# Channel-norm variance in four column groups of 32, root and reciprocal over 128 partitions

## What is computed

```
x1 = depthwise_conv3x3(x) + dw_b                   # NHWC: 128 channels last
mu = x1.mean(-1, keepdims=True)
var = ((x1 - mu) ** 2).mean(-1, keepdims=True)     # one value per pixel, over 128 channels
x1 = (x1 - mu) / jnp.sqrt(var + LN_EPS) * ln_g + ln_b
x1 = jax.nn.gelu(x1, approximate=False)
offset = x1 @ off_w + off_b                        # and a softmax mask, also from x1
```

## Time and profile before

| | |
|---|---|
| median of 3 runs | 10189.35 us (10180.25 to 10204.99) |
| the profiled execution | 10212.5 us |
| its span, first to last instruction | 10210.4 us |
| mean granted clock of TensorE, 1 is full speed | 0.891 |
| period of a sample in the loop | about 590 to 604 us |

### The profile page before, as it was taken

One profiled execution on the slowest core, in us unless ns is written; L12 is line 12 of the kernel. 1 busy time (PEld: TensorE's weight loads), 2 busy tenths in 40 slices (PEclk: granted clock), 3 DMA queues, 4 the chain that ended last, 5 costly groups with the idle time before them and its releaser, 6 DMA issues.

```text
span 10210.4 us, 287594 instructions
## 1 busy us (share of the span) xinstructions
PE 8259.8 (81%) x123582; PEld 4592.7 (45%) x123582; DVE 7412.6 (73%) x8864; ACT 3945.7 (39%) x6092; POOL 211.1 (2%) x253
## 2 busy tenths in 40 slices
PE   6468888887888888788888878888887888888796
PEld 5324435353444535344343535434353443535354
DVE  2487777778777776877777687777768777786863
ACT  0034434253443425344342534435253443435332
POOL 0000000000000000000000000000000000000000
PEclk7579898998989899899989989899998989899898
DMA  4001101111110111111011111101111110111101
GB/s 111 6 13 35 47 20 45 37 37 39 41 47 20 45 37 37 39 41 47 20 45 37 37 39 41 47 20 45 37 37 39 41 46 20 45 32 43 41 24 52
DMA packets 230313, 391.71 MB, mean 38 GB/s; under 512 B 25200, under 2 KB 166480, under 8 KB 221776
## 3 DMA queue, kind: packets, MB, share of 16 engines
q1 hardware_dynamic: 229008, 372.66, 13.1%
HBM read 192.47 MB, written 130.55 MB: 32 GB/s over the span
## 4 chain that ended last, share of the span: by engine, by line
PE 58%; DVE 22%; issue 11%; ACT 7%; DMA 1%; DVEq 0%; POOL 0%; SPq 0%; ACTq 0%; POOLq 0%
PE ps L881 10%; PE ps L686 7%; PE ps L750 7%; DVE arena L1703 4%; PE ps L783 4%; PE ps L981 4%; PE ps L758 3%; PE ps L799 3%; PE ps L971 3%; DVE arena L1758 3%; PE ps L707 3%; PE ps L772 2%; DVE arena L1680 2%; DVE arena L1686 1%; DVE arena L1798 1%
## 5 line engine op out<-in xcount | busy, mean ns | idle before, releaser
L881 PE MATMUL ps<-arena,ident 64*64 64x512 f32 x5600 | 1761.5, 679 | 743.5 <-DVE arena L1703 740.4
L883 PE MATMUL ps<-arena,ident 48*64 48x512 f32 x5600 | 1765.5, 679 | 0.0
L1703 DVE TENSOR_TENSOR arena<-arena 112x2560 f32<-112x2560 f32 x560 | 1578.4, 2820 | 99.5 <-PE ps L883 93.1
L881 PEld LDWEIGHTS ps<-arena,ident 64*64 64x64 f32 x5600 | 493.2, 148 | 1785.1 <-issue 1774.4
L750 PE MATMUL ps<-arena,wqk 128*128 128x400 f32 x2048 | 926.9, 572 | 170.8 <-DVE arena L1807 108.5
L686 PE MATMUL ps<-vp,convw 128*128 128x448 f32 x2016 | 819.5, 549 | 23.6 <-ACT vp L1300 23.6
L1792 DVE COPY arena<-ps 128x400 f32<-128x400 f32 x512 | 293.3, 573 | 728.3 <-PE ps L750 728.1
L1686 DVE TENSOR_TENSOR arena<-arena 112x576 f32<-112x576 f32 x1008 | 764.1, 758 | 34.9
L799 PE MATMUL ps<-arena 64*64 64x33 f32 x32768 | 652.6, 230 | 116.4 <-issue 58.8
L783 PE MATMUL ps<-ident,arena 128*128 128x128 f32 x4096 | 594.9, 292 | 150.9 <-ACT arena L1097 43.7
L1798 DVE TENSOR_REDUCE arena<-ps 128x16 f32<-128x800 f32 x512 | 505.2, 987 | 282.2 <-PE ps L772 278.0
(11 more groups left out here) (294 smaller groups left out, 12637.3 us busy)
## 6 DMA issues: line engine op xcount, KB each, us to landing
windows_out<-arena SPq DMA_DIRECT2D x1024, 100.0 KB
arena<-windows_out SPq DMA_DIRECT2D x224, 256.0 KB, 4.1
arena<-windows_out SPq DMA_DIRECT2D x224, 192.0 KB, 3.4
arena<-in_wqk SPq DMA_DIRECT2D x16, 2048.0 KB, 8.5
arena<-in_x_t SPq DMA_DIRECT2D x16, 1568.0 KB, 10.1
arena<-in_x SPq DMA_DIRECT2D x16, 1568.0 KB, 7.7
arena<-arena SPq DMA_DIRECT2D x32, 784.0 KB
out_x<-xb SPq DMA_DIRECT2D x112, 224.0 KB, 2.0
```

Source lines behind the costliest of these rows:

```text
L881: nc.tensor.matmul(ps[half, 3, :], ident[0:SLOT, 0:SLOT], prod[0:SLOT, ring(c, dy), dx, :], start=(s < 2), stop=(s >= TAPS - 2), skip_grou ...
L883: mm = nc.tensor.matmul(ps[half, 4, :], ident[SLOT:PT, SLOT:], prod[SLOT:PT, ring(c, dy), dx, :], start=(s < 2), stop=(s >= TAPS - 2), ski ...
L1703: V.tensor_tensor(prod[0:PT, ring(c, dy), :, :].rearrange("p k (n e) -> p k n e", e=CG), taps.to_broadcast([PT, SHIFTS, N64, CG]), for_tap ...
```

## The change

The seven variance matmuls no longer write seven partitions of one tile. Chunk k writes to the 32 partitions from 32 (k % 4), the column group k % 4. The weight is one of two 128x32 matrices: for chunks 0 to 3 the columns 0 to 15 hold 1/128 and the rest zero, for chunks 4 to 6 the columns 16 to 31. So each variance row exists 16 times, and chunk k's is at partition 32 (k % 4) + 16 (k // 4). Chunks 0 to 3 start the accumulation in their column group, chunks 4 to 6 add to it; group 3 has chunk 3 alone, and its other 16 partitions hold zero.

The square root and the reciprocal go over all 128 partitions. The spread matmul of chunk k contracts over the 32 partitions of its quarter, with the one-hot column of `ident` that picks the row. Order, semaphores, banks, and the number of matmuls stay.

```diff
-        varsel = sb("varsel", [C, CHUNKS, CHUNKS])
+        varsel = sb("varsel", [C, 2, 32])
...
             def spread_rows(n, k, bank):
                 pe.wait_ge(ln_r.sem, ln_r.at(n))
-                nc.tensor.matmul(ps[:, bank, 0:CH], ident[0:CHUNKS, k:k + 1].to_broadcast([CHUNKS, C]),
-                                 var_rows[0:CHUNKS, :], start=True, stop=True).then_inc(bc_p.sem, 1)
+                quarter, at = slice(32 * (k % 4), 32 * (k % 4) + 32), 32 * (k % 4) + 16 * (k // 4)
+                nc.tensor.matmul(ps[:, bank, 0:CH], ident[quarter, at:at + 1].to_broadcast([32, C]),
+                                 var_rows[quarter, :], start=True, stop=True).then_inc(bc_p.sem, 1)
...
                     for k in range(CHUNKS):
-                        mm = nc.tensor.matmul(ps[0:CHUNKS, 5, 0:CH], varsel[:, k, :], y1[:, k * CH:(k + 1) * CH],
-                                              start=(k == 0), stop=(k == CHUNKS - 1))
+                        quarter = slice(32 * (k % 4), 32 * (k % 4) + 32)
+                        mm = nc.tensor.matmul(ps[quarter, 5, 0:CH], varsel[:, k // 4, :], y1[:, k * CH:(k + 1) * CH],
+                                              start=(k < 4), stop=(k >= 3), skip_group_check=True)
                     mm.then_inc(ln_v.sem, 1)
...
                     act.wait_ge(ln_v.sem, ln_v.at(n))
-                    nc.scalar.activation(sd_rows[0:CHUNKS, :], ps[0:CHUNKS, 5, 0:CH], ACT.Sqrt, bias=eps_col[0:CHUNKS, :]
-                                         ).then_inc(ln_d.sem, 1)
+                    nc.scalar.activation(sd_rows, ps[:, 5, 0:CH], ACT.Sqrt, bias=eps_col[:, :]).then_inc(ln_d.sem, 1)
...
-            V.memset(varsel[:, :, :].rearrange("p a b -> p (a b)")[:, 0:CHUNKS * CHUNKS:CHUNKS + 1], 1.0 / C)
+            for hv in range(2):
+                V.memset(varsel[:, hv, 16 * hv:16 * hv + 16], 1.0 / C)
...
                     dve.wait_ge(ln_d.sem, ln_d.at(n))
-                    V.reciprocal(var_rows[0:CHUNKS, :], sd_rows[0:CHUNKS, :]).then_inc(ln_r.sem, 1)
+                    V.reciprocal(var_rows, sd_rows).then_inc(ln_r.sem, 1)
```

## The result

| | before | after |
|---|---|---|
| median of the runs | 10190.6 us (4 runs, 10180 to 10205) | 10057.0 us (4 runs, 10053 to 10121) |
| ratio of after to before, 95% interval | | 0.9883 (0.9841 to 0.9924) |
| profiled execution: span, mean granted clock | 10210.4 us, 0.891 | 10051.0 us, 0.903 |

134 us less, 1.3%.

A forecast was written before the change was run, and what follows sets the result against it. TensorE was taken to lead (81% busy), alone in the variance step. Direct gain 15 x 3.7 + 4.0 + 2.2 = 61.7 us plus 87 us of clock falls, off the median 10189.35, gave 10041 us; range 9995 to 10145.

The forecast's parts named there:

- Variance step: Fourteen variance matmul passes, four column groups at once: 5.43 to 1.67 us, counted as 3.7 us less per sample.
- The table load: Before the square root: its 1.28 us load delays the root, so the matmul waiting on it starts at most 0.3 us later.
- The estimate from the Trainium skill's figure for three groups: Variance step: 2.38 times faster, 5.36 to 2.3 us, 3.1 us less per sample, 46 us over 15 samples.
- Root and reciprocal over 128 partitions: Square root and reciprocal after the variance step: 128 instead of 7 partitions cost between 0 and 0.05 us.
- Sample 0: First sample, at low clock: variance step 4.0 us less, three spread pairs 2.2 us less.
- The falls behind spread steps, 87 us: Spread steps: with 32 rows the clock falls go, 28.5 steps times 3.06 us (10.45 - 7.39); bounds 0 and 87.
- Few rows, not idleness: Spread steps: clock falls follow matmuls with few active rows (7), not few columns and not idle time; basis of the 87 us.
- The long spells: Half clock before or at the first spread step, 8 of 15 samples, up to 5.69 us more; taken as not touched.
- The slower rival: Clock falls after the shortened variance step until the first spread step, 7.1 us a sample: 10233 us; chance 4%.
- Other signs: Profile after the change: spread steps of 7.4 us, granted clock 1.00 in all of them.

The follow-up runs named there:

- the kernel with the split reciprocal: Kernel before with only its reciprocal in two parts, 300 of 448 columns ahead of VectorE's copy of step 19, 148 at the old place: 10107 us (0.9918).

## Why the prediction was right, and where it was not

- **Variance step, 5.43 to 1.67 us.** Measured 1.70 to 2.14, mostly 1.70. Four column groups under 128 rows run fully side by side. The 15 samples gave 56.4 us on the way to the first spread step against 55.5 forecast (55 in the means of two). The table load did cover the root as worked out: L785 waits 0.34 us for it where 0.3 was forecast (sample 7).
- **What a rule would have given.** The estimate from the Trainium skill's figure for three groups ("TensorE: Matmul & The Clock Gate", "Measured speedup vs the span model"), 46 us, was too low. The ratio here is 5.43 to 1.70, 3.2 times for seven matmuls in four groups; the measurement decides.
- **Root and reciprocal over 128 partitions.** Forecast 0 to 0.05 us, measured 0.008 and 0.012.
- **Sample 0.** Forecast 6.2 us less, measured 6.8.
- **The falls behind spread steps, 87 us.** That more rows take these falls away was right: rows without groups bring it. The size was off. The term was 28.5 steps times 10.45 - 7.39, and 27.5 of them, 84 us, were second and third steps. These gave 50 us. The floor is not 7.39 but 8.3 in the second and third step, because ScalarE loads two tables there; the first step, from which I took 7.39, has no GELU behind it. The trace of before had this floor to read: sample 1's second and third step run at a clock of 1.00 and take 8.31 us each. And a third step still has a fall in 10 of 15 samples.

```profile
1046.79:1055.10 8.31, 7.47 (x153) 1.00 0.09 27
1055.10:1063.41 8.31, 7.70 (x154) 1.00 0.09 26
```

- **"Few rows, not idleness".** This reading of the falls was half right. With 7 rows kept and only the idle time behind the reciprocal cut, no second step has a fall. Both count here, and the sentence that idleness has no part in them doesn't stand.
- **The long spells, which I left out of the sum.** "One spell is not touched", I wrote, and that was wrong. The first step gave 47 us: 44 because eight long spells of the trace before don't occur in the trace after, and 3 for sample 10's fall, which the 87 had in them. I had allowed a few either way. The repeated executions have five before and three after, so the first pair overstates it; in the means of two the first step gave 33 us. That is not all chance either: 24 of 60 samples without groups have such a spell, and 6 of 60 with them.
- **The total.** In the means of two the second and third step fall short of the forecast by some 36 us, and the first step gives some 30 more than forecast. The two nearly cancel. That the total came out near is in part luck.
- **The base.** The median of before is what I subtracted from, but the steps were counted in an execution 20 us above it. The two profiled executions of before lie 15 us above their medians in the mean, those of after 1 below. Between the profiled ones the means of two are 151 us apart, 142 of them in the stretch and sample 0, and 134 between the medians.
- **The slower rival,** a fall between the variance step and the first spread step in every sample, did not show: 1 sample of 15 in the first execution, 5 in the second. As a sign that the prediction is wrong, a low clock there says little: the two executions of before have it in 8 and 5 samples.
- **Other signs.** I had said that spread steps take 7.4 us and that the clock is at 1.00 in all of them. The first does; the second takes 8.3, and the third still falls in most samples.

## What to carry to other kernels

Read the granted clock by step, and set steps of equal work side by side: here it showed that thin matmuls (7 rows of the array) were followed by half-clock spells although TensorE was hardly idle. Giving such a matmul more rows cost next to nothing: four passes took 1.76 us with 7 rows, 1.75 with 32 and 1.85 with 128, and at full clock the second step took 8.3 us with all three. More rows here meant fewer falls. Idle time of 2 us ahead of them mattered as well. Before counting what a step at full clock costs, take one with the same work on all engines, not its neighbour. And profile both kernels twice when the clock moves, and set each profiled execution against the median of its runs: 24 and 11 us lay between two executions of the same kernel in this one stretch.

## What the runs showed of the hardware

- Four column groups of 32 under all 128 rows, fp32 operands, 448 columns: in sample 15 the second, third and fourth round of four passes start 0.40, 0.376 and 0.376 us after the one before, and single passes started 0.376 us apart before. Four different moving operands of 128 partitions at once cost nothing measurable.
- The clock's falls went with the rows of the spread matmuls, at the same passes and columns of these matmuls: sums of 302 to 308 us for 30 steps with 7 rows, 293 with 8, 255 to 261 with 32, 249 with 128. Seven columns under 128 rows were not followed by a fall. Yet in the kernel with the split reciprocal 7 rows gave 269, so rows are not all of it.
- A piece of TensorE's idle time of 1.66 to 2.07 us behind the reciprocal is followed by a long half-clock spell in some samples and not in others: 8, 5, 7 and 4 of 15 without groups, and 6 of the 25 such samples with groups, with 7, 8 or 32 rows in the spread. Behind pieces of at most 1.41 us none of 35 samples has one. With 128 rows the clock was back within the spread matmuls.
